# Perceiver block: self-attention's projections as three f16 products of high and low halves

## The reference

```
q, k, v = LN(x) Wq, ctx Wk, ctx Wv                      # 16 heads of 32
x = x + softmax(q k^T / sqrt(32), mask) v Wo            # cross-attention, 8192 keys
z = LN(x)
a_q, a_k = softplus(z Wq_amp^T), softplus(z Wk_amp^T)   # per head divided by its root mean square
p_q, p_k = pi tanh(z Wq_phi^T), pi tanh(z Wk_phi^T)
s = (a_q cos p_q . a_k cos p_k + a_q sin p_q . a_k sin p_k) / sqrt(32) * exp(score_log_scale), causal
x = x + softmax(s) (z Wv^T) Wo^T                        # self-attention, 512 keys
x = x + top-2-of-16 experts on LN(x), 64 rows per expert and batch entry
```

## Time and profile before

| | |
|---|---|
| median of 3 runs | 2141.32 us (2140.72 to 2145.28) |
| profiled execution, its own time | 2142.47 us |
| its span | 2140.7 us |
| mean granted PE clock | 0.969 |
| PE, DVE, ACT, POOL busy | 1966.8, 1748.2, 1512.3, 44.3 us |
| the chain that ended last: PE, DVE, issue, DMA | 80, 8, 4, 4% |

### The profile page before, as it was taken

One profiled execution on the slowest core, in us unless ns is written; L12 is line 12 of the kernel. 1 busy time (PEld: TensorE's weight loads), 2 busy tenths in 40 slices (PEclk: granted clock), 3 DMA queues, 4 the chain that ended last, 5 costly groups with the idle time before them and its releaser, 6 DMA issues.

```text
span 2140.7 us, 30896 instructions
## 1 busy us (share of the span) xinstructions
PE 1966.8 (92%) x11354; PEld 794.9 (37%) x11354; DVE 1748.2 (82%) x1657; ACT 1512.3 (71%) x1918; POOL 44.3 (2%) x58
## 2 busy tenths in 40 slices
PE   7799999999999998999999999999888999985493
PEld 3233333333333333333333333333224444443382
DVE  5589999999999998799999999999975676665244
ACT  2388888888888886688888888888843555552020
POOL 2000000000000000000000000000000000000203
PEclk9899999999999999999999999999999999998697
DMA  5533323333233332133323333223300000021884
GB/s 189 190 104 94 90 79 89 89 94 94 75 89 91 92 101 87 50 90 89 94 75 94 90 89 99 75 84 77 131 21 1 1 1 1 1 89 32 283 280 143
DMA packets 112586, 194.55 MB, mean 91 GB/s; under 512 B 10288, under 2 KB 63536, under 8 KB 112432
## 3 DMA queue, kind: packets, MB, share of 16 engines
q1 hardware_dynamic: 109872, 184.12, 29.2%
q0 software_dynamic: 2560, 8.39, 1.2%
HBM read 108.58 MB, written 50.33 MB: 74 GB/s over the span
## 4 chain that ended last, share of the span: by engine, by line
PE 80%; DVE 8%; issue 4%; DMA 4%; ACT 2%; POOL 1%; SPq 1%; POOLq 0%; ACTq 0%; DVEq 0%
PE ps L964 21%; PE ps L1082 20%; PE ps L882 11%; PE ps L879 11%; PE ps L989 5%; PE ps L1145 3%; DVE dacc L1483 2%; PE ps L1017 2%; PE ps L952 1%; PE ps L1155 1%; DMA kscr<-wsm 1%; PE ps L995 1%; PE ps L1045 1%; PE ps L1030 1%; DMA kst<-kscr 1%
## 5 line engine op out<-in xcount | busy, mean ns | idle before, releaser
L1319 ACT ACTIVATE pt<-ps,bias 128x1024 f32<-128x1024 f32 x1024 | 1109.4, 1114 | 222.5 <-PE ps L1082 221.3
L1483 DVE TENSOR_TENSOR dacc<-dacc,pt 128x2048 f32<-128x2048 f32 x504 | 1152.9, 2288 | 49.0 <-ACT pt L1319 22.9
L1082 PE MATMUL ps<-qst,kst 128*128 128x512 f16 x2048 | 615.1, 383 | 19.8 <-ACT pt L1319 19.0
L964 PE MATMUL ps<-pt,vt 128*32 128x512 f32 x4096 | 495.4, 601 | 0.0
L1082 PEld LDWEIGHTS ps<-qst,kst 128*128 128x128 f16 x2048 | 178.3, 98 | 423.9 <-ACT pt L1319 131.3
L879 PE MATMUL ps<-wsm 128*128 128x512 f16 x1152 | 315.0, 384 | 14.8 <-DVE wsm L1440 10.8
L882 PE MATMUL ps<-wsm 128*128 128x512 f16 x1152 | 310.8, 380 | 5.5 <-ACT vt L1200 2.9
L964 PEld LDWEIGHTS ps<-pt,vt 128*32 128x32 f32 x4096 | 107.1, 109 | 263.6 <-issue 243.1
L879 PEld LDWEIGHTS ps<-wsm 128*128 128x128 f16 x1152 | 113.5, 99 | 157.8 <-issue 10.8
L882 PEld LDWEIGHTS ps<-wsm 128*128 128x128 f16 x1152 | 112.4, 98 | 145.2 <-issue 4.2
L1284 ACT ACTIVATE pr<-ps,nmx 128x128 f32<-128x128 f32 (+3 forms) x128 | 66.4, 523 | 117.0 <-DVE nmx L1585 116.7
(11 more groups left out here) (186 smaller groups left out, 1250.6 us busy)
## 6 DMA issues: line engine op xcount, KB each, us to landing
kscr<-wsm SPq DMA_DIRECT2D x128, 256.0 KB, 3.5
kst<-kscr SPq DMA_DIRECT2D x128, 256.0 KB, 3.4
kst<-kst SPq DMA_DIRECT2D x128, 256.0 KB, 3.4
wsm<-in_ctx SPq DMA_DIRECT2D x32, 768.0 KB, 4.7
qst<-qscr SPq DMA_DIRECT2D x32, 128.0 KB, 2.9
xbuf<-xn SPq DMA_DIRECT2D x16, 256.0 KB, 6.6
wsm<-in_gate SPq DMA_DIRECT2D x8, 512.0 KB, 5.0
wsm<-in_fc SPq DMA_DIRECT2D x8, 512.0 KB, 5.9
```

What stands on the lines that cost most here:

```text
L964: p = e.matmul(ps[32 * h:32 * h + 32, 4 + n % 2, :], vt[:, kb % 2, ch, c:c + 32], pt[:, (2 * i + h // 2) % 6, h % 2, :], start=ch == 0, st ...
L1082: p = e.matmul(ps[:, 2 * half + h2, :], kst[:, kb % 2, h, ch * 128:ch * 128 + 128], qst[:, h, :], start=True, stop=True)
L1319: e.activation(pt[:, (2 * i + half) % 6], ps[:, 2 * half:2 * half + 2, :], ACT.Exp, bias=bias[:, 4 * kb + ch:4 * kb + ch + 1], scale=SCORE ...
L1483: e.tensor_tensor(own_heads, own_heads, probs, ALU.add).then_inc(S["add"], 1)
```

## The change

- The activations and the weights of the five products are scaled (by 16 and 64), and each is held as an f16 high half and an f16 low half (the rest). A product of a 128-row chunk is now three f16 products: high x high, high x low, low x high. PSUM holds 1024 times the result; the readers scale by `UNIT`.
- `wsm` holds the f16 halves (`whl`). The f32 weights are loaded to three places that the last block no longer uses (two in the first half of `kst`, one in that of `vt`), the fourth and fifth load behind the split of an earlier weight in the same place. Pool splits each by three instructions over 128x2048 (times 64, cast, subtract), semaphore `wsp`.
- `xT2` has two halves: ACT writes the high one (`copy`), DVE the low one (new piece `low`, slot 7; for tile 0 before the add of step 511).
- `amp` is two DVE instructions: `relu` (scale and max with 0, from PSUM, slot 2, for tile 0 slot 3) and an add.
- `xn` of tile 0 moves from step 500 to step 509 and waits for two split weights. SP waits for all five before it loads `wo2`. Buffers of the stage are laid out in another order.
- The semaphores `mask` and `zeros` go: the second half of `x` and the mask share one, and the memset of `att` stands before the bias.

```diff
+CHUNKS = [(c, xi, wi) for c in range(4) for xi, wi in ((0, 0), (0, 1), (1, 0))]
...
+        if slot == (3 if begun else 2):
+            out.append(("relu", t))
...
                 out.append(("copy", t + 1))
+                out.append(("low", t + 1))
...
+        whl = wf_.bitcast(F16).rearrange("p (a b c d) -> p a b c d", a=5, b=2, c=4)
+        staged = [x.rearrange("p a b -> p (a b)").bitcast(F32) for x in (kst[:, 0, 0:8], kst[:, 0, 8:16])]
+        staged.append(vt[:, 0].rearrange("p a b -> p (a b)"))
...
                 if i == 496:
...
-                    for w, n in enumerate(("wqa", "wka", "wqp", "wkp", "wv2")):
-                        e.dma_start(wsm[:, w], A[n].rearrange("(k p) n -> p k n", p=128)).then_inc(S["ws"], 16)
+                    e.wait_ge(S["sc"], 2 * 496)
+                    stage(0, "wqa")
+                    stage(1, "wka")
+                    e.wait_ge(S["av"], 496)
+                    stage(2, "wqp")
+                    e.wait_ge(S["wsp"], 1)
+                    stage(0, "wkp")
+                    e.wait_ge(S["wsp"], 3)
+                    stage(2, "wv2")
...
             choose(e, "sp")
+            e.wait_ge(S["wsp"], 5)
...
+            e.wait_ge(S["unit"], 256)
+            for x in range(4):
+                e.wait_ge(S[f"kw{x}"], 16 * 32)
+            for n, at, loaded in ((0, 0, 3), (1, 1, 3), (2, 2, 4), (3, 0, 4), (4, 2, 5)):
+                hi, lo = (whl[:, n, k].rearrange("p c d -> p (c d)") for k in range(2))
+                e.wait_ge(S["ws"], 16 * loaded)
+                e.tensor_scalar(staged[at], staged[at], WS, None, ALU.mult).then_inc(S["pool"], 1)
+                e.wait_ge(S["pool"], d.up())
+                e.tensor_copy(hi, staged[at]).then_inc(S["pool"], 1)
+                e.wait_ge(S["pool"], d.up())
+                e.tensor_tensor(lo, staged[at], hi, ALU.subtract).then_inc(S["wsp"], 1)
...
-                        e.wait_ge(S["ws"], 80)
+                        e.wait_ge(S["wsp"], w0 + lo // 12 + 1)
                         e.wait_ge(S["ex"], 2 * STEPS)
                     for m in range(lo, hi):
-                        n, k = m // 4, m % 4
-                        p = e.matmul(ps[:, w0 + n, :], xT2[:, t % 2, k * 128:k * 128 + 128], wsm[:, w0 + n, k, :],
-                                     start=k == 0, stop=k == 3)
+                        n, (c, xi, wi) = m // 12, CHUNKS[m % 12]
+                        p = e.matmul(ps[:, b0 + n, :], xT2[:, t % 2, xi, c * 128:c * 128 + 128], whl[:, w0 + n, wi, c, :],
+                                     start=m % 12 == 0, stop=m % 12 == 11)
...
-                    e.activation(xT2[:, i, :], ps[:, 0, :], ACT.Copy).then_inc(S["xTs"], 1)
+                    e.activation(xT2[:, i, 0], ps[:, 0, :], ACT.Copy, scale=XS).then_inc(S["xTh"], 1)
...
             e.memset(hpi[:], PI / 2)
+            e.memset(att[:, 0, :], 0.0)
...
-                    e.scalar_tensor_tensor(out=amp[:, i, :], in0=pair(0), scalar=0.0, in1=t1[:], op0=ALU.max,
-                                           op1=ALU.add).then_inc(S["amp"], 1)
+                    e.wait_ge(S["dve"], relu)
+                    e.tensor_tensor(amp[:, i, :], amp[:, i, :], t1[:], ALU.add).then_inc(S["amp"], 1)
+                elif what == "relu":
+                    e.wait_ge(S["mag"], t + 1)
+                    e.tensor_scalar(amp[:, i, :], pair(0), UNIT, 0.0, ALU.mult, ALU.max).then_inc(S["dve"], 1)
+                    relu = own.up()
+                elif what == "low":
+                    e.wait_ge(S["xTh"], t + 1)
+                    e.scalar_tensor_tensor(out=xT2[:, i, 1], in0=ps[:, 0, :], scalar=XS, in1=xT2[:, i, 0], op0=ALU.mult,
+                                           op1=ALU.subtract).then_inc(S["xTs"], 1)
...
-                if i == 500:
+                if i == 509:
+                    e.wait_ge(S["wsp"], 2)
                     self_piece(("xn", 0))
...
+                if i == STEPS - 1:
+                    self_piece(("low", 0))
                 adds(i)
```

More of the change, by code:

```diff
@@ L21 @@
 SCORE = 1.0 / (KS * KS * ROOT)
+XS = 16.0
+UNIT = 1.0 / (XS * WS)
 BIG = 3.4028234663852886e38
@@ L188, in pe @@
         p.then_inc(f["pe"], 1)
-        e.wait_ge(f["act"], s_b.at("act", 0, 1))
+        e.wait_ge(f["dve"], s_b.at("dve", 0, 2))
         for w0 in (0, 2):
-            for m in range(8):
-                n, k = w0 + m // 4, m % 4
-                p = e.matmul(ps[:, n, :], xT2[:, 0, k * 128:k * 128 + 128], wsm[:, n, k, :], start=k == 0, stop=k == 3)
+            for m in range(24):
+                n, (c, xi, wi) = w0 + m // 12, CHUNKS[m % 12]
+                p = e.matmul(ps[:, n, :], xT2[:, 0, xi, c * 128:c * 128 + 128], whl[:, n, wi, c, :], start=m % 12 == 0,
+                             stop=m % 12 == 11)
             p.then_inc(f["pe"], 1)
@@ L259, in dve @@
                         ALU.mult).then_inc(f["dve"], 1)
+        e.wait_ge(f["act"], s_b.at("act", 0, 1))
+        e.scalar_tensor_tensor(out=xT2[:, 0, 1], in0=ps[:, 0, :], scalar=XS, in1=xT2[:, 0, 0], op0=ALU.mult,
+                               op1=ALU.subtract).then_inc(f["dve"], 1)
         end(e)
@@ L548 @@
 SEMS = """const
- wk wv x0 x1 wq mask late zero wo2
- c0 c1 qw0 qw1 qw2 qw3 ql0 ql1 ql2 ql3 kw0 kw1 kw2 kw3 kr0 kr1 kr2 kr3 ku0 ku1 ku2 ku3 ws
+ wk wv x0 x1 wq late zero wo2
+ c0 c1 qw0 qw1 qw2 qw3 ql0 ql1 ql2 ql3 kw0 kw1 kw2 kw3 kr0 kr1 kr2 kr3 ku0 ku1 ku2 ku3 ws wsp
  pool dve act hi0 chi lo0 wsplit split var root norm n1 xt xTc qry qlo unit khi klo vev maxs max1 bias esl
- sc ex add av oac fin dnc dnx okr att prj x2 flagm flag zeros
- xn turn xTs p01 abs amp p23 p4 sv ms mroot msr phi tabs sin cos polar qkT QT KT
+ sc ex add av oac fin dnc dnx okr att prj x2 flagm flag
+ xn turn xTh xTs p01 mag abs amp p23 p4 sv ms mroot msr phi tabs sin cos polar qkT QT KT
  score nmx prob scale pT tcD tcA value aT wom x3 lvar lroot lstat xn3 rT rC rM lg
@@ L773, in sp, with stage @@
                 if i == 496:
[L774 to L777, removed]
-                    for w, n in enumerate(("wqa", "wka", "wqp", "wkp", "wv2")):
-                        e.dma_start(wsm[:, w], A[n].rearrange("(k p) n -> p k n", p=128)).then_inc(S["ws"], 16)
+                    def stage(at, name):
+                        e.dma_start(staged[at].rearrange("p (k n) -> p k n", k=4),
+                                    A[name].rearrange("(k p) n -> p k n", p=128)).then_inc(S["ws"], 16)
+                    e.wait_ge(S["sc"], 2 * 496)
[7 more added lines that the diff above has]
+                    stage(2, "wv2")
                 if ch == 3 and kb == 15:
@@ L1238, in self_piece @@
                         e.wait_ge(S["cos"], t)
-                    e.activation(t1[:], pair(0), ACT.Abs).then_inc(S["act"], 1)
-                    absolute = own.up()
+                    e.activation(t1[:], pair(0), ACT.Abs, scale=UNIT).then_inc(S["mag"], 1)
                 elif what == "exp":
-                    e.wait_ge(S["act"], absolute)
+                    e.wait_ge(S["mag"], t + 1)
                     e.activation(t1[:], t1[:], ACT.Exp, scale=-1.0).then_inc(S["act"], 1)
@@ L1249, in self_piece @@
                     e.wait_ge(S["p4"], t + 1)
-                    e.activation(sv[:, t, :], ps[:, 1, :], ACT.Copy).then_inc(S["sv"], 1)
+                    e.activation(sv[:, t, :], ps[:, 1, :], ACT.Copy, scale=UNIT).then_inc(S["sv"], 1)
                 elif what == "mroot":
@@ L1259, in self_piece @@
                         e.wait_ge(S["sin"], t)
-                    e.activation(phi[:], pair(1), ACT.Tanh).then_inc(S["phi"], 1)
+                    e.activation(phi[:], pair(1), ACT.Tanh, scale=UNIT).then_inc(S["phi"], 1)
                     if t:
```

56 lines of the change are left out of this document (25 added, 31 removed).

## The result

Median 2164.38 us (2162.66 to 2169.84) against 2141.02 us for the kernel before on the same chip: ratio 1.0109, 95% interval 1.0087 to 1.0131. Slower, as forecast, by 23 us instead of 37. The profiled execution took 2162.66 us.

A forecast was written before the change was run, and what follows sets the result against it. DVE was taken to limit the last key block and PE the eight-tile stage. 2142.5 + 52 (Pool against adds) - 16 (tile stage) + 0.5 (start) = 2179, as a median 2178 us, range 2121 to 2192.

The forecast's parts named there:

- Two-operand adds and Pool shut each other out: Last key block: DVE's adds with two SBUF operands and Pool's split take turns in full; chance 0.47, +52 us.
- The upper bound: Cost of Pool beside DVE's adds in the last block, bounded at 0 and full exclusion; full exclusion taken, +52 us.
- the block of 105 us: Sign of taking turns: last block some 105 us, with adds of 5 to 8 us or gaps before them.
- 58 us of Pool work: Last block: Pool's split takes 11.6 us a weight, 58 us for five, 66 at the upper end.
- +52 us: Last block: with Pool and DVE taking turns, the stretch to add 508 lasts 85 us instead of 33.1.
- The count of 16 partners up to step 508: Last block: 10 adds and 6 two-operand finish instructions of DVE take turns with 15 Pool instructions.
- Weights ready before PE asks: Under full exclusion, all five split weights are ready before PE asks for them.
- Tile 0, -1.65 predicted: Tile 0: 0.8 us won before the sum of the last denominators and 0.85 on the value product.
- Tile stage, -14.8 predicted: First score to last values: PE's f16 savings less DVE's added low halves and relu passes, -14.8 us.
- Nothing for the value products: Tiles 1 to 7: 28 value products' saving, 6.0 us, counted as nothing since PE waits behind them for ACT's exponential.
- the 112 products: Tiles 1 to 7: amplitude and phase products, where PE has no gap, save 23.9 us.
- The clock, which "should change little": PE's clock, 0.97 in the tile stage, should change little; more low stretches would eat the gain.

The follow-up runs named there:

- experiment 1: Changed kernel with Pool's three split instructions per weight replaced by memsets of the same places, so the weights are zero: 2125.64 us.
- experiment 2: Changed kernel keeping only Pool's multiplication of each weight, its cast and subtraction replaced by memsets: 2142.63 us (one run).
- experiment 8: Kernel of experiment 1 with the value product issued twice in all eight tiles: 2129.92 us.
- experiment 5: Changed kernel with the weight split still in the last block, but ACT making the high halves and DVE the low ones, Pool nothing: 2136.41 us.

## Why the prediction was right, and where its sizes were off

*Two-operand adds and Pool shut each other out: right.* The upper bound was chosen because no row cleared a second SBUF operand, a choice given 0.47, and the lists show the two engines taking turns; experiment 1 shows that it takes Pool instructions that read. Of the signs named, adds of 5 to 8 us came (5.5 to 6.0 beside a multiplication or a subtraction) and the block of 105 us didn't (89.8): the direction and the mechanism were right, and the cost was 20 us in the span where 36 was summed. The Trainium skill, "SBUF — State Buffer", section "Who interferes with whom", says so of the pair, and has a GpSimd instruction that only writes not compete; the 1806 ns memsets beside unslowed adds agree. Its statement that the loser waits for the whole instruction agrees with the subtraction (3.93 us, held to the end) and not with the f32 multiplication (3.3 of 5.2 us).

*58 us of Pool work: right.* Once running, the three take 5.2, 1.9 and 3.9 us against the 5.5, 1.9 and 4.1 worked out from 128 and 512 columns: 55 for the five against 58. Pool began at 1529.5 instead of 1532.6, of which 2.8 is the earlier block.

*+52 us: the term that was mis-sized, by 14.* It took every Pool instruction for as long as it lasts, less the 6 us of PSUM-fed instructions that fit beside them. Taking from each DVE record of the block its undisturbed length gives what really was held. Each of the fifteen Pool instructions held exactly one:

| Pool instruction, x5 | its own time | DVE held |
|---|---|---|
| multiplication | 26.1 | 15.6 |
| cast | 9.1 | 7.5 |
| subtraction | 19.6 | 14.3 |
| sum | 54.9 | 37.4 |

Pool's work was 3 us shorter than 58. Four multiplications let DVE in 3.3 to 3.5 us after they began to run (experiment 2 shows it for this instruction alone), 1.9 us early each: 7.6. The fifth held xn(0), with one tensor operand, for 4.4 us, to within 0.3 of its end. The remaining some 4 us are mostly PSUM-fed instructions of DVE that ran beside Pool beyond the 6 counted. The count of 16 partners up to step 508 failed too: by the end of add 508, 62.5 us after Pool's start (85 predicted), Pool had finished 12 of the 15, and the last three held DVE behind it.

*Weights ready before PE asks: right.* The last was ready at 1605.3; PE waited nowhere for Pool.

*Tile 0, -1.65 predicted and +2.1 measured: wrong, in three terms.* The sum of the denominators was to start 0.8 us earlier behind the last add. PE had idled 13.4 us behind held adds, waited 1.16 us more for the low half, and took 4.59 us, at a granted clock of 0.59, for 12 products that take 2.75 further on at 1.00; the sum started 2.42 us behind the add (1612.29 to 1614.71) where it was 2.00. In experiment 1, with nothing held, it started 0.66 behind the add: there the term was right. Seven relu passes were costed; the eighth stands here, in front of xn(1), for which PE waits: with it, and 0.4 us more behind the flag, DVE had xn(1) ready 7.6 us after PE's transpose of the flag instead of 5.9 (+1.7), while PE had 1.4 us less to do: a wait of 3.78 us instead of 0.69. Behind that wait the same 4 f32 products (8 records) took 5.87 instead of 3.60 us (+2.3), at a granted clock of 0.61 instead of 1.00. The last part isn't the block's doing: in experiment 1, with an undisturbed block and the first 12 products in 2.76 us, PE waited 4.58 us there and the 4 took 6.07.

*Tile stage, -14.8 predicted and -16.5 measured: the sum right, its terms not.* That the sum came out is in part luck, since errors of both signs lie in it. Nothing for the value products agrees with the profile of experiment 8, but its medians leave up to some 4 us open; `relu` at half its time should have been nothing, `low` 1.9 instead of 4.8. With 23.9 for the 112 products counted in full that would make 22.0; 5.5 of it didn't come. The f16 products ran at their 0.215 us (12 in 2.75), yet PE's busy time fell by 25.9 us where 140 products of 0.215 less are 30.1; the granted clock of the stage reads 0.95 instead of 0.96. PE's idle time rose by 9.4 where 6.0 for the value products and 1.9 for `low` make 7.9; the waits that grew are those for ACT (+4.8) and for DVE's copies `pT` (+3.1). Which of the products fell into them wasn't tried. (The 0.86 us for an f32 product is right by the rows of 8 records in 3.60 us; from the 12 in 5.42 that the prediction names, it would be 0.875.)

*The clock, which "should change little": wrong in the last block.* It was granted 0.72 there and 0.957 over the whole, against 0.94 and 0.969 before. In the tile stage it held, at 0.95 against 0.96.

*The memset at the start, +0.5: nothing.* It ran at 79.59 us, in a place where DVE waited for PE anyway, and the first copy came at 86.27 against 86.47.

## What to carry to other kernels

An idle Pool isn't free where its instructions read SBUF beside DVE instructions that take two operands from there: count its work as DVE's, unless DVE has as much room in that stretch. The same split on Pool cost 38 us beside a full DVE, and nothing that shows spread over the 200 steps before; the room of the stretch, not the engine's idleness, is what to look up. ACT, in experiment 5, read SBUF beside the same adds and held none. And a pass that is hidden in seven tiles of a pipeline can be bare in the first, so each added instruction is to be placed once in the prologue too.

## What the runs showed of the hardware that wasn't expected

- Pool's f32 times a scalar over 2048 columns shut out DVE's two-operand adds for only 3.3 of its 5.2 us; its subtraction (3.93) held them to its end.
- A DVE instruction whose only tensor operand is in SBUF, as its result, isn't safe: xn(0), 128x512, took 4.98 us instead of 0.54, and ran from 0.3 us before the end of Pool's multiplication. In experiment 2 it took 1.21 us and ran from 0.3 us before the end of a memset of Pool, where the adds lose nothing to memsets. It is one case of each.
- Held time is inside the records (5.53 for an add of 2.29; 7.40 for a multiplication of 5.2), so that DVE looks 98% busy in a block of 89.8 us in which 37 of them are waiting. Only the mean of a group against its mean elsewhere shows it.
- Neither engine starved: with adds back to back, each Pool instruction waited for one DVE instruction at most (2.2 us), and each add for one Pool instruction.
- PE's products slow down behind idle stretches: the granted clock was 0.72 in the block after, with 40.7 of 89.8 us idle, against 0.94 before, and 0.50, the lower of the two levels (1.2 GHz), for the 5.8 us behind the wait of 13.4. But the price of a short wait doesn't go by its length. The 4 products of tile 0, 3.60 us behind a wait of 0.69 before, took 4.59 to 6.19 us in the twelve profiled kernels with the changed tile 0, behind waits of 1.9 to 4.8 us and in no order (5.14 behind the shortest, 4.65 behind the longest).
- The reverse shows in the one profile of experiment 8: with 84 more products in the tile stage its granted clock was 0.98 instead of 0.95, and they cost PE 11.2 us of busy time instead of 18.1.
